# Experts of a decoder layer: gate and up with the weights stationary, in 39 steps of 256 rows, weights fetched per step

## What is computed

```python
x = x + mamba(layernorm(x)); x = x + cross_attention(layernorm(x), ctx)
h = layernorm(x).reshape(-1, 256)                       # 4096 tokens
probs = softmax(h @ gate_w.T)                           # 8 experts
topw, sel = top_k(probs, 2);  topw = topw / sum(topw)
combine = sum(one_hot(sel, 8) * topw[..., None], axis=1)
gate, up = split(einsum('th,efh->etf', h, gate_up_w))   # 256 -> 2 x 1024
hact = up * gelu(gate)
expert_out = einsum('etf,ehf->eth', hact, down_w)       # 1024 -> 256
out = x + einsum('eth,te->th', expert_out, combine)
```

## Time and profile before

| | us |
|---|---|
| median of 3 runs | 2240.38 (2240.24 to 2242.9) |
| the profiled execution | 2242.78 |
| its span, first to last instruction | 2240.9 |
| first product of the experts, start | 1417.94 |
| last product of the experts, end | 2233.45 |
| mean granted clock of TensorE | 0.955 of full speed |

### The profile page before, as it was taken

One profiled execution on the slowest core, in us unless ns is written; L12 is line 12 of the kernel. 1 busy time (PEld: TensorE's weight loads), 2 busy tenths in 40 slices (PEclk: granted clock), 3 DMA queues, 4 the chain that ended last, 5 costly groups with the idle time before them and its releaser, 6 DMA issues. The chain is left out here.

```text
span 2240.9 us, 30635 instructions
## 1 busy us (share of the span) xinstructions
PE 1980.2 (88%) x9858; PEld 1380.8 (62%) x9859; DVE 1252.0 (56%) x1717; ACT 1094.8 (49%) x1843; POOL 1059.6 (47%) x783
## 2 busy tenths in 40 slices
PE   6889999999989898668777883899999999999998
PEld 2666777676767677445555553466666666666665
DVE  4899999999999888356777657211111111111111
ACT  3898989899898987113333330122222222222221
POOL 1787878787878878044544432222222222222221
PEclk8999999999999999688999996999999999999999
DMA  4011302121211110300110016112221211111111
GB/s 127 13 58 38 88 30 92 38 67 39 67 39 57 57 39 20 102 0 0 38 45 21 20 38 241 30 22 79 80 80 23 80 23 21 23 23 23 22 24 19
DMA packets 77382, 109.13 MB, mean 49 GB/s; under 512 B 11569, under 2 KB 56113, under 8 KB 75234
## 3 DMA queue, kind: packets, MB, share of 16 engines
q1 hardware_dynamic: 63618, 89.16, 12.5%
q0 software_dynamic: 13664, 18.69, 5.1%
HBM read 85.42 MB, written 22.41 MB: 48 GB/s over the span
## 5 line engine op out<-in xcount | busy, mean ns | idle before, releaser
L237 POOL TENSOR_TENSOR m_hc_ring<-m_h_ring,m_c_bc 128x1024 f32<-128x1024 f32 x256 | 606.2, 2375 | 123.9 <-DVE m_h_ring L398 105.5
L1597 PE MATMUL e_ps<-w,e_xT 128*128 x1136 | 513.9, 595 | 1.6 <-ACT e_xT L1527 1.1
L282 ACT ACTIVATE m_a_ring<-m_delta,m_negA 128x512 f32<-128x512 f32 x512 | 365.8, 715 | 40.9 <-DVE m_h_ring L398 40.4
L1570 DVE TENSOR_TENSOR e_hact<-e_gact,e_ps 128x512 f32<-128x512 f32 x142 | 97.7, 688 | 509.5 <-ACT e_gact L1532 509.5
L489 PE MATMUL m_ps<-m_ident,m_bxT 128*128 128x128 f32 x2048 | 320.9, 280 | 61.6 <-DVE m_h_ring L398 56.3
L489 PEld LDWEIGHTS m_ps<-m_ident,m_bxT 128*128 128x128 f32 x2048 | 235.2, 141 | 210.7 <-DVE m_h_ring L398 97.6
L294 ACT ACTIVATE m_bxT<-m_uT,m_bT 128x512 f32<-128x512 f32 x512 | 364.1, 712 | 0.0
L1597 PEld LDWEIGHTS e_ps<-w,e_xT 128*128 128x128 f32 x1136 | 205.9, 191 | 208.2 <-issue 208.2
L398 DVE TENSOR_TENSOR_SCAN m_h_ring<-m_a_ring,m_carry,m_ps 128x512 f32<-128x512 f32 x256 | 316.5, 1267 | 27.8 <-ACT m_a_ring L282 13.1
L398 DVE TENSOR_TENSOR_SCAN m_h_ring<-m_a_ring,m_ps 128x512 f32<-128x512 f32 x256 | 303.7, 1208 | 35.8 <-ACT m_a_ring L282 12.9
L506 PE MATMUL m_ps<-m_ident,m_hc_ring 128*128 128x128 f32 x2048 | 308.2, 274 | 2.6 <-POOL m_hc_ring L237 1.7
(11 more groups left out here) (195 smaller groups left out, 2388.3 us busy)
## 6 DMA issues: line engine op xcount, KB each, us to landing
m_c_bc<-c_rows SPq DMA_DIRECT2D x32, 1024.0 KB, 6.0
w<-in_gate_up_w SPq DMA_DIRECT2D x16, 1024.0 KB, 6.4
w<-in_down_w SPq DMA_DIRECT2D x8, 1024.0 KB, 10.5
m_x_in<-in_x SPq DMA_DIRECT2D x8, 512.0 KB, 5.7
m_x_res<-in_x SPq DMA_DIRECT2D x8, 512.0 KB, 6.8
x<-m_x_res SPq DMA_DIRECT2D x8, 512.0 KB, 2.8
t_xa<-x SPq DMA_DIRECT2D x8, 512.0 KB, 4.0
out<-t_xa SPq DMA_DIRECT2D x8, 512.0 KB, 3.0
```

The costliest lines, as they stand in the source:

```text
L237: p.tensor_tensor(hc_ring[:, k % HC, :, :], h_ring[:, n % 2, e:e + 2, :], c_bc[:, n, :].unsqueeze(1).to_broadcast([P, 2, CT]), ALU.mult).t ...
L282: a.activation(a_ring[:, k % A_RING, :], delta[:, c % 2, e, :], ACT.Exp, scale=negA[:, e, n:n + 1]).then_inc(a_ready, 1)
L1570: nc.vector.tensor_tensor(hact[:, j % 2, h * BANK:(h + 1) * BANK], gact[:, h, :], ps[:, 2 * h + 1, :], ALU.mult).then_inc(h_ready, 1)
L1597: last = t.matmul(ps[:, 2 * h + which, :], xT[:, j % 2, c, :], w1[:, bass.ds(slot, 1), c, lo:lo + BANK].rearrange("p a n -> p (a n)"), sta ...
```

## The change

Tiles come in pairs of one expert. The dispatch starts each expert at a multiple of 256 rows (a shift by 8), so that 39 pairs (`PAIRS`), 78 tiles, always hold the list; all 39 steps run. The table is now only the expert of each step, 39 numbers, and DVE makes it before it builds the places (4 instructions moved ahead of the turns; the 9 small ones behind them are gone).

In `gate_up`, slices of 128 channels of `w1` are stationary and 256 tokens of `xT` move. Gate and up come out with channels on partitions, in four groups per step of two banks each; DVE writes its product straight into `hT`, and `turn_h` with its transposes and copies is gone. `down` does for each of the two tiles what it did for one, and waits only for the products' `h_ready`. PSUM holds two groups of gate and up and two banks for the result.

All eight `w2` are loaded once in the dispatch. `w1` is loaded anew for every step into a ring of six buffers (`load_w1`): SP reads the step's expert from the table, and issues two transfers of 1 MB. Six steps are requested in the dispatch, with no wait between them but that for the table; step s later, when the last group of step s-6 is done. POOL gathers and scatters two tiles per step, without the copies of row numbers. The program of the experts is written out for all steps, with no loop.

```diff
-LOADS = 48
+PAIRS = 39
+STEPS = PAIRS
+W1_RING = 6
 
 def mamba_phase(nc, x, in_w, conv_w, xproj_w, dtproj_w, dtproj_b, a_log, d_vec, out_w, ident_c, c_rows_dram, x1):
...
-            for e in range(SLOTS):
-                load_weights(sp, e, e, gate_up_w, down_w, w1, w2, w_loaded)
+            for e in range(E):
+                sp.dma_start(w2[:, e, :, :], down_w[e].rearrange("(c p) d -> p c d", p=P)).then_inc(w2_loaded, 16)
+            sp.wait_ge(tabled, 1)
+            for s in range(W1_RING):
+                load_w1(sp, s, tables, gate_up_w, w1, w1_loaded)
...
+            then(v.tensor_scalar(nt_f[:], upto[:, NT - 1, :], float(2 * P - 1), None, ALU.add))
...
+            then(v.tensor_copy(pairs[:], nt_i[:]))
+            then(v.tensor_tensor_scan(pend[:], ones[:, 0:E], pairs[:], 0.0, ALU.mult, ALU.add))
+            wide = [1, PAIRS, E]
+            then(v.tensor_tensor(passed[:], iota[0:1, 0:PAIRS].unsqueeze(2).to_broadcast(wide),
+                                 pend[0:1, :].unsqueeze(1).to_broadcast(wide), ALU.is_ge))
+            then(v.reduce_sum(eid[:], passed[:], AXX))
+            then(v.tensor_scalar(eid[:], eid[:], float(E - 1), None, ALU.min))
+            v.tensor_copy(tables[:], eid[:]).then_inc(tabled, 1)
...
-            then(v.tensor_tensor(passed[:], iota[0:1, 0:TILES].unsqueeze(2).to_broadcast([1, TILES, E]),
-                                 tend[0:1, :].unsqueeze(1).to_broadcast([1, TILES, E]), ALU.is_ge))
-            then(v.reduce_sum(eid[:], passed[:], AXX))
-            then(v.tensor_scalar(eid[:], eid[:], float(E - 1), None, ALU.min))
-            then(v.tensor_copy(expert_i[:], eid[:]))
...
-            then(v.tensor_copy(tables[:, 2, 0:E], need[:, 0:E]))
...
+def load_w1(sp, s, tables, gate_up_w, w1, w1_loaded):
+
+    E, D = gate_up_w.shape[0], gate_up_w.shape[1]
+    e = sp.value_load(tables[0:1, s:s + 1], min_val=0, max_val=E - 1)
+    for c in range(D // P):
+        sp.dma_start(w1[:, s % W1_RING, c, :],
+                     gate_up_w[bass.ds(e, 1), c * P:(c + 1) * P, :].rearrange("a p f -> (a p) f")).then_inc(w1_loaded[s % W1_RING], 16)
...
+    X_RING = 3
+
+    tiles_of = [(2 * k, 2 * k + 1) for k in range(PAIRS)]
+    TILES = tiles_of[-1][-1] + 1
+    chunks_of = [KF // 4 if len(tiles) == 2 else KF // 2 for tiles in tiles_of]
+    groups_of = [KF // n for n in chunks_of]
...
-        T_BANK, Y_BANK, X_BANK = 4, 6, 7
+        Y_BANK, X_BANK = 4, 6
...
+        def gu_bank(s, g, which):
+            return ps[:, 2 * ((first_group[s] + g) % 2) + which, :]
+
+        def h_out(s, g):
+            n = chunks_of[s]
+            return hT[:, s % 2, g * n:(g + 1) * n, 0:len(tiles_of[s]) * P]
...
-            sp.sem_inc(y_done, ONE)
-            for e in range(SLOTS, E):
-                end = sp.value_load(tables[0:1, 2, e - SLOTS:e - SLOTS + 1], min_val=1, max_val=TILES + 1)
-                sp.wait_ge(y_done, end)
-                load_weights(sp, e, e % SLOTS, gate_up_w, down_w, w1, w2, w_loaded)
+            for s in range(W1_RING, STEPS):
+                sp.wait_ge(gu_done, first_group[s - W1_RING + 1])
+                load_w1(sp, s, tables, gate_up_w, w1, w1_loaded)
...
+            def gather(s):
+                if s >= X_RING:
+                    pool.wait_ge(x_turned, s - X_RING + 1)
+                for i, tile in enumerate(tiles_of[s]):
+                    nc.gpsimd.indirect_dma_start(
+                        out=xg[:, s % X_RING, i, :], out_offset=None, in_=xn2,
+                        in_offset=bass.IndirectOffsetOnAxis(ap=ids[:, tile:tile + 1], axis=0)).then_inc(x_loaded[s % X_RING], 16)
+
+            def scatter(s):
+                pool.wait_ge(y_ready, s + 1)
+                for i, tile in enumerate(tiles_of[s]):
+                    if tile:
+                        pool.wait_ge(added, 16 * tile)
+                    nc.gpsimd.indirect_dma_start(
+                        out=out, out_offset=bass.IndirectOffsetOnAxis(ap=ids[:, tile:tile + 1], axis=0),
+                        in_=y[:, s % 2, i, :], in_offset=None, compute_op=ALU.add).then_inc(added, 16)
+
+            for s in range(X_RING - 1):
+                gather(s)
+            for s in range(STEPS):
+                if s + X_RING - 1 < STEPS:
+                    gather(s + X_RING - 1)
+                scatter(s)
...
+            def gelu(s, g):
+                k = first_group[s] + g
+                act.wait_ge(gu_done, k + 1)
+                if k >= 2:
+                    act.wait_ge(h_ready, k - 1)
+                nc.scalar.activation(gact[:, k % 2, :], gu_bank(s, g, 0), ACT.Gelu).then_inc(g_ready, 1)
+
+            turn_x(0)
+            for s in range(STEPS):
+                gelu(s, 0)
+                if s + 1 < STEPS:
+                    turn_x(s + 1)
+                for g in range(1, groups_of[s]):
+                    gelu(s, g)
 
...
+            def times_up(s, g):
+                k = first_group[s] + g
+                dve.wait_ge(g_ready, k + 1)
+                if s >= 2 and g == 0:
+                    dve.wait_ge(y_done, s - 1)
+                n = chunks_of[s]
+                nc.vector.tensor_tensor(h_out(s, g), gact[:, k % 2, :].rearrange("p (f t) -> p f t", f=n),
+                                        gu_bank(s, g, 1).rearrange("p (f t) -> p f t", f=n),
+                                        ALU.mult).then_inc(h_ready, 1)
...
+            def weigh(s):
+                dve.wait_ge(y_done, s + 1)
+                if s >= 2:
+                    dve.wait_ge(added, 16 * (tiles_of[s - 2][-1] + 1))
+                for i, tile in enumerate(tiles_of[s]):
+                    last = nc.vector.tensor_scalar(y[:, s % 2, i, :], ps[:, Y_BANK + s % 2, i * D:(i + 1) * D],
+                                                   weights[:, tile:tile + 1], None, ALU.mult)
+                last.then_inc(y_ready, 1)
+
+            for s in range(STEPS):
+                times_up(s, 0)
+                if s:
+                    weigh(s - 1)
+                for g in range(1, groups_of[s]):
+                    times_up(s, g)
+            weigh(STEPS - 1)
...
+            def turn_x(s):
+                n = len(tiles_of[s])
+                pe.wait_ge(x_loaded[s % X_RING], 16 * loads_of[s])
+                if s:
+                    pe.wait_ge(xT_ready, s)
                 for c in range(KD):
-                    last = t.transpose(ps[:, X_BANK, c * P:(c + 1) * P], xg[:, j % U, c * P:(c + 1) * P], ident[:])
+                    for i in range(n):
+                        last = t.transpose(ps[:, X_BANK, (c * n + i) * P:(c * n + i + 1) * P],
+                                           xg[:, s % X_RING, i, c * P:(c + 1) * P], ident[:])
                 last.then_inc(x_turned, 1)
...
+            def gate_up(s, g):
+                k = first_group[s] + g
+                n, wide = chunks_of[s], len(tiles_of[s]) * P
+                if k >= 2:
+                    pe.wait_ge(h_ready, k - 1)
+                for f in range(n):
+                    for which in range(2):
+                        lo = which * F + (g * n + f) * P
+                        for c in range(KD):
+                            last = t.matmul(gu_bank(s, g, which)[:, f * wide:(f + 1) * wide],
+                                            w1[:, s % W1_RING, c, lo:lo + P],
+                                            xT[:, s % 2, c, 0:wide], start=(c == 0), stop=(c == KD - 1))
                 last.then_inc(gu_done, 1)
...
-            def turn_h(i, j, h):
-                pe.wait_ge(h_ready, 2 * i + h + 1)
-                if not (isinstance(i, int) and i == 0):
-                    pe.wait_ge(hT_ready, 2 * i + h - 1)
-                for c in range(KF // 2):
-                    lo = h * BANK + c * P
-                    last = t.transpose(ps[:, T_BANK + h, c * P:(c + 1) * P], hact[:, j % 2, lo:lo + P], ident[:])
-                last.then_inc(h_turned, 1)
...
+            def down(s):
+                e = pe.value_load(tables[0:1, s:s + 1], min_val=0, max_val=E - 1)
+                if s == 0:
+                    pe.wait_ge(w2_loaded, 16 * E)
+                pe.wait_ge(h_ready, first_group[s + 1])
+                if s >= 2:
+                    pe.wait_ge(y_ready, s - 1)
+                for i in range(len(tiles_of[s])):
+                    for f in range(KF):
+                        last = t.matmul(ps[:, Y_BANK + s % 2, i * D:(i + 1) * D], hT[:, s % 2, f, i * P:(i + 1) * P],
+                                        w2[:, bass.ds(e, 1), f, :].rearrange("p a n -> p (a n)"),
+                                        start=(f == 0), stop=(f == KF - 1))
                 last.then_inc(y_done, 1)
 
-            def entry(k, i, most):
-                return pe.value_load(tables[0:1, k, bass.ds(i, 1)], min_val=0, max_val=most)
-
-            turn_x(0, 0, 0)
-
-            def tile(i, g, j, first, last):
-                slot = entry(0, i, SLOTS - 1)
```

(49 more changed lines are left out.)

162 lines of the change are left out of this document (30 added, 132 removed).

## The result

The changed kernel takes 2260.24 us, median of 4 runs (2258.31 to 2263.91); the kernel before, 2240.31, median of 4 (2237.84 to 2242.9). The ratio is 1.0091, with a 95% interval of 1.0073 to 1.0108: 19.9 us slower. The profiled execution took 2261.15 us, its span 2259.3.

The account below looks back on a forecast made before the run. PE was taken to bound the kernel. Experts' stretch +15.5, dispatch +2.8, start +3.8 and tail +4.5 sum to +26.6 us on the median of 2240.38, giving 2267 us, range 2260 to 2277.

Parts of the forecast that it names:

- the sum's own range: Whole kernel: 2262 (quiet gather, records 0.4% under `down`'s rate) to 2272 us (a few groups that wait).
- the core of the sum: Experts: padding to 256 rows costs 74.2 us, more than the 58.2 us saved by removing transposes; +16.0 us.
- the one at 2255 to 2261: Whole kernel: tables and start cost nothing and new records come out 1% shorter (8 us); chance 0.06.
- PE's work for a pair: Experts, one step: 13.84 gate and up, 6.92 `down`, 0.44 `turn_x`; 21.20 us where two tiles were 22.84.
- Other engines beside PE: Experts: DVE, ACT, loads and POOL stay beside PE's steps and add zero.
- Dispatch: Dispatch: table instructions moved ahead of the turns and wider turns add 2.8 us, bounds +2 to +3.5.
- Cold clock: First 16 expert records: PE idles as long beforehand as it did, so the same 3.1 us are lost.
- Start of the experts: Before the experts' first product: gather slowed by queued loads, plus wider transposes and copy; +3.8 us, from +0.6.
- the collision: Start of the experts: the first gather falls beside 20 MB of queued loads, landing after 6.0 us; +3.2 us.
- The two small terms: Start of the experts: second gather, taken as no net cost; two more transposes and a wider copy, +0.6 us.
- Tail: Behind PE's end: a second scaling (+0.5) and a second scatter-add after the first (+3.8 + 0.2); +4.5 us.
- Rival of the load queue: Dispatch end: SP stalls issuing loads, last one after 1413, and holds the barrier; 2270 to 2274 us, chance 0.12.

Follow-up runs that it names:

- e1: The kernel before with only each expert's start aligned to 256 rows, 78 tiles instead of 71, old products and loop kept: 2320.96 us.
- e2: The changed kernel with 35 steps instead of 39, enough for these inputs but not for any inputs: 2172.43 us.
- e5: The changed kernel with the eight `w2` loads issued behind the six steps of `w1` loads in the dispatch: 2273.45 us.
- e4: The changed kernel with 71 steps of one 128-row tile, gate and up weights still stationary, no padding to 256: 2200.19 us.
- e6: e4 with every gate and up product cut into two of 64 columns, each with its own weight load: 2725.57 us.
- b2: The changed kernel with 32 steps of 256 rows and 8 of 128 instead of 39 pairs: 2201.68 us, ratio 0.9838 to the kernel before.

## Why the prediction came out right, and which terms did not

**Forecast and sign.** 2260.24 us lies inside the range of 2260 to 2277, but by 0.24 us, and two of the four runs are under it; it is also under the sum's own range of 2262 to 2272. That the range held is luck; the sign and the core of the sum are not. Under 2262 the prediction had only another case, the one at 2255 to 2261 with a chance of 0.06, in which tables and start cost nothing and the records come out 1% shorter. The measured time falls among its values, but only its cheap start came true: the dispatch did cost 2.7, and the records were 0.2% shorter. The change is slower for the reason forecast. The core of the sum, 3.5 more pairs of 21.2 us against 1.64 us saved per pair, is what `e1` takes apart, +82 for the padding and -61 for the rest, and `e2` gives the price of a step. From `e2`, 19.9 us over is 0.94 of a step: with 38 steps, which wouldn't hold every list, the change would have been even.

**PE's work for a pair: nearly.** I took `down`'s rate of 0.2163 us per 256-column record; it is 0.2159, and the step 21.155 us instead of 21.20. On 39 steps that is 1.8 us of the missing 6.7.

**Other engines beside PE: right.** One wait in 830 us, the 1.5 us for the last `hT` that the prediction had. Steps written out showed no wait for instructions either. By the Trainium skill, Runtime: NRT & Kernel Launch, section Instruction fetch mechanics, the fetch of straight code is mostly hidden; the trace of after agrees, with 600.00 us busy of 600.00.

**Dispatch: right,** +2.7 against +2.8.

**Cold clock: right.** The first 16 records took 6.67 us instead of the 3.45 of later ones, +3.2 against the 3.1 taken over; the granted clock was 0.52 from 1415 to 1425, near the level of 1.2 GHz.

**Start of the experts: this is the step that failed,** +0.4 instead of +3.8, half of the whole miss. The forecast first product at 1424 to 1425 came at 1418.59: 3.4 of this by the start, and 2.4 because the phases ahead were shorter. The prediction let 20.97 MB run at 314 GB/s until 1426 and slowed the gather beside them. That rate was read from a stretch in which SP waited for each expert's 3 MB to land before it requested the next. Cut finer, the kernel before shows it:

```profile
1370.00:1375.00 5.00, 0.14 (x1) 0.00 (x0) 4.17 (x18) 0.00 (x0) 0.00 (x0) 0.50 0.68 231
1375.00:1380.00 5.00, 0.00 (x0) 0.00 (x0) 4.62 (x13) 0.00 (x0) 0.75 (x1) 0.50 1.02 384
```

SP requests at 1359.3, 1370.6 and 1381.2; the rate falls to 231 GB/s around such a gap and is 384 within. The mean of 314 had the gaps in it, and the new queue has none (the changed kernel, the same columns):

```profile
1410.00:1412.00 2.00, 0.00 (x0) 0.00 (x0) 0.42 (x2) 0.00 (x0) 0.50 (x1) 1.00 1.02 426
1412.00:1414.00 2.00, 0.00 (x0) 0.00 (x0) 0.00 (x0) 0.00 (x0) 1.40 (x3) 1.00 0.47 174
```

The queue moves 426 GB/s up to 1412 and runs empty within the next microsecond: 20.97 MB in some 56 us, 376 GB/s in the mean (351 while `w2` runs, 412 and more with `w1`). The first gather is issued at 1412.57, just then, the second at 1413.91, and PE starts 2.8 us behind the second, the landing time of a quiet gather. The size that I gave the collision, +3.2, was right at worst; only it didn't happen here. It does in `e5`, +3.1, and in part where a shorter dispatch lets the first gather meet the end of the queue: in `e2` it is issued at 1407.36 and the queue runs to some 1410, +1.7; in `e4` it is issued at 1413.67, with 438 GB/s from 1413 to 1415, and lands after 4.5 us instead of 2.8. So this kernel is on the edge of that cost: anything that makes the dispatch shorter gives part of the gain back, and the kernel of 128 rows pays it already. The two small terms nearly cancel: the second gather added 0.3 that I had at zero, and of the 0.6 for wider transposes and copy 0.06 are left. They did take 0.65 more, but PE followed the copy's end after 0.14 us instead of 0.73. The figure of the Trainium skill, DMA: Bandwidth & Descriptors, section Bandwidth, which the prediction set aside, was the nearer one: 425 GB/s there, 421 to 426 here while `w1` alone was loaded (1390 to 1412). It holds for `w1`'s rows of 8 KB; `w2`, in rows of 1 KB, came at 348 to 359.

**Tail: an upper estimate.** +3.5 instead of +4.5. The two scalings take 0.88 us together instead of 0.48 twice, POOL then issues 1.15 us after their start instead of 1.28, and the second scatter-add starts 3.77 after the first, not 4.0.

**Rival of the load queue: a real mechanism that did not decide.** SP does stall, which the trace of before could not show. The eight loads of `w2` in the changed kernel (durations of the issue, min/median/max ns, then time to landing):

```profile
L1287 SPq DMA_DIRECT2D w<-in_down_w x8: 463/2922/2936, 1356.9 to 1371.8; - x8
...
DMA to landing us min/median/max: 5.9/11.9/12.0
```

The third issue takes 1.85 us and from the fourth on each takes 2.92 to 2.94, just the time of one such load (1.05 MB at 359 GB/s): the fourth ends at 1362.9, when the first load has landed (5.9 us after 1356.9). But these stalls end at 1375, and the twelve loads of `w1` are issued by 1390.9, some 20 us before the barrier and far from the 1413 that I had named as the sign of this rival. It is decided by when the loads can start and which come last: `e5` changes both and pays 12.4 us.

## What to carry to other kernels

Count the padded rows before counting the saving per row: a wider step must win more on every step than its rounding adds. Here 256 rows instead of 128 bought 0.5 us per pair of tiles and cost seven tiles; the rest of the change, without it, is a gain of 1.9%. A record can be narrowed until its time stops falling, here at 128 columns, and that width was the best of those tried for ragged groups. And where loads are to be queued ahead of a barrier, start with those that wait for nothing and end with those that the queue takes without a stall, since the issuing engine itself can be what the barrier waits for; here the first were also those in short rows, and no run tells the two rules apart.

## What the runs showed of the hardware that I had not expected

- At full clock the records of gate and up take no less than 0.111 us on average: 64 columns 0.1113 (`e6`), 128 columns 0.1117 (`e4`), 256 columns 0.2159; the 8-column ones of the expert choice take 0.112. The weight load's row shows 190 to 192 ns all the while, so that number is no spacing. Transposes of 128 columns, with load rows of 141 ns, take 0.110.
- The granted clock can stay at 0.50 while PE has no gap: for 40 us, nearly all in 64-column records, in `e6`. And 2.2 us of waiting in the middle of the experts (`b2`) brought it from 1.00 to 0.52, at 1.6 us on top of the wait.
- SP's issue of a 1 MB load in rows of 1 KB stalls from the third on (1.85 us, then 2.92 each), and once for 18.6 us behind twelve loads in rows of 8 KB (`e5`).
- Loads in rows of 8 KB moved 411 to 426 GB/s in windows of 5 us, in rows of 1 KB 348 to 359, with the DMA engines' share at 1.0 and above in both, whichever came first (`after`, `e5`).
